# Reciprocal roots of the heads' norms: one power on GpSimd in place of a first guess and three Newton steps on VectorE

## The reference

```python
def _rms_norm(t):
    ms = jnp.mean(t * t, axis=-1, keepdims=True)
    return t * jax.lax.rsqrt(ms + RMS_EPS)
...
h = _layernorm(x, axis=-1) * (1 + ca) + sa
q, k, v = ...        # 16, 4 and 4 heads of 16 channels
q = _rms_norm(q)
k = _rms_norm(k)
attn = softmax(q k^T * scale)
y = attn v
vn = v / jnp.maximum(jnp.linalg.norm(v, axis=-1, keepdims=True), L2_EPS)
y = y - jnp.sum(y * vn, axis=-1, keepdims=True) * vn
x = x + ga * (y Wo)
h = _layernorm(x, axis=-1) * (1 + cb) + sb
x = x + gb * ffn(h)  # 8 experts, those with the top 0.9 of the probability
```

## Time and profile before

| | |
|---|---|
| median of 3 runs | 515.72 us (515.63 to 517.07) |
| profiled execution | 515.67 us, span 513.9 us |
| PE busy | 459.1 us, 89% of the span |
| DVE busy | 340.0 us, 66% |
| ACT busy | 257.9 us, 50% |
| POOL busy | 196.4 us, 38% |

### The profile page before, as it was taken

The page is one execution under the profiler, slowest core; times in us unless marked ns, Lnnn a source line. Parts: engine busy times, 40 slices in busy tenths (PEclk is TensorE's granted clock), DMA queues, the critical chain, the costliest instruction groups (busy, mean ns, idle before and its releaser), DMA issues. The chain is left out here.

```text
span 513.9 us, 9827 instructions
## 1 busy us (share of the span) xinstructions
PE 459.1 (89%) x3390; PEld 346.9 (67%) x3390; DVE 340.0 (66%) x789; ACT 257.9 (50%) x355; POOL 196.4 (38%) x233
## 2 busy tenths in 40 slices
PE   3855998999999999999998999989998999999982
PEld 3433334344444444443898999989997999999982
DVE  3388577469857986768899857764743847555451
ACT  2313677975787588777543243444422525333330
POOL 1036204002100210002243575655754665676644
PEclk9966799999999999999999898999999999999997
DMA  8500231921001100213346347774653674454443
GB/s 267 193 1 0 51 76 17 111 39 41 2 1 42 43 1 1 84 37 99 115 119 192 64 106 187 189 202 96 176 104 63 133 169 74 106 83 107 75 73 41
DMA packets 30784, 46.00 MB, mean 89 GB/s; under 512 B 3588, under 2 KB 22276, under 8 KB 30728
## 3 DMA queue, kind: packets, MB, share of 16 engines
q0 software_dynamic: 11936, 22.50, 24.1%
q1 hardware_dynamic: 18792, 22.77, 13.8%
HBM read 34.44 MB, written 12.93 MB: 92 GB/s over the span
## 5 line engine op out<-in xcount | busy, mean ns | idle before, releaser
L609 ACT ACTIVATE probs<-psS 128x1024 f32<-128x1024 f32 x128 | 123.2, 1027 | 23.9 <-PE psS L1403 23.4
L1636 PE MATMUL psS<-hs_hi,w_hi 128*128 128x256 f32 x400 | 115.4, 288 | 5.7 <-DVE hs_lo L1194 3.2
L1636 PE MATMUL psS<-hs_hi,w_lo 128*128 128x256 f32 x400 | 113.9, 285 | 0.0
L1636 PE MATMUL psS<-hs_lo,w_hi 128*128 128x256 f32 x400 | 113.8, 285 | 0.0
L474 POOL DMA_INDIRECT out<-y_sel,idx_out x44 | 77.4, 1759 | 36.2 <-DVE y_sel L1231 24.7
L1636 PEld LDWEIGHTS psS<-hs_hi,w_hi 128*128 128x128 f32 x400 | 77.0, 193 | 7.6 <-issue 7.6
L1636 PEld LDWEIGHTS psS<-hs_lo,w_hi 128*128 128x128 f32 x400 | 76.9, 192 | 0.0
L1636 PEld LDWEIGHTS psS<-hs_hi,w_lo 128*128 128x128 f32 x400 | 76.7, 192 | 0.0
L460 POOL DMA_INDIRECT h_sel<-h_rows,idx_in x50 | 54.0, 1080 | 53.1 <-DVE sel L1200 21.7
L1502 PE MATMUL psY<-probs,v_aug 128*32 128x512 f32 x512 | 69.3, 613 | 0.0
L395 POOL COPY parted<-parted 128x512 f32<-128x512 f32 x16 | 10.0, 627 | 135.8 <-DVE parted L848 135.8
(11 more groups left out here) (200 smaller groups left out, 725.8 us busy)
## 6 DMA issues: line engine op xcount, KB each, us to landing
w_in<-gateT SPq DMA_DIRECT2D x8, 512.0 KB, 4.8
w_in<-upT SPq DMA_DIRECT2D x8, 512.0 KB, 3.5
w_in<-downT SPq DMA_DIRECT2D x8, 512.0 KB, 4.4
h_rows<-h_nat SPq DMA_DIRECT2D x4, 528.0 KB, 3.5
x_all<-x SPq DMA_DIRECT2D x4, 512.0 KB, 5.4
h_rows<-mod_table POOLq DMA_DIRECT2D x4, 512.0 KB, 14.7
out<-x_all SPq DMA_DIRECT2D x4, 512.0 KB, 3.0
mod_rows<-mod_table SPq DMA_DIRECT2D x3, 512.0 KB, 5.0
```

The costliest lines, as they stand in the source:

```text
L609: act.activation(probs[:, gk % 4, 2 * pair:2 * pair + 2, :], psS[:, pair, :, :], ACT.Exp, scale=ATT_SCALE).then_inc(probs_done, 1)
L1636: mm = pe.matmul(ps[:, i * SW:(i + 1) * SW], w, v[:, k, :], start=at == 0, stop=at == 3 * KC - 1)
```

## The change

`reciprocal_roots` becomes `floor_norms`: DVE makes only the two small operations that scale the mean and set the floors. Then GpSimd raises all 96 columns to the power -0.5 in one instruction, with a tile `minus_halves` of as many exponents, and DVE's `split_heads` waits for it. GpSimd has the power ahead of the doubling of the same batch's parts.

```diff
-            def reciprocal_roots(b):
-
+            def floor_norms(b):
 
                 dve.tensor_scalar(norms[:, :, 0:HG], norms[:, :, 0:HG], 1.0 / D, RMS_EPS,
-                                  ALU.mult, ALU.add).then_inc(newton_step, 1)
+                                  ALU.mult, ALU.add).then_inc(floored, 1)
                 dve.tensor_scalar(norms[:, :, HG:ALLH], norms[:, :, HG:ALLH], L2_EPS_SQUARED, None,
-                                  ALU.max).then_inc(newton_step, 1)
-                z, y, t = (norms[:, :, :].rearrange("p t h -> p (t h)"), rnorm[:, :, :].rearrange("p t h -> p (t h)"),
-                           newton[:, :])
-                at = b * 13 + 2
-                dve.wait_ge(newton_step, at)
-                dve.tensor_scalar(t.bitcast(I32), z.bitcast(I32), 1, None, ALU.logical_shift_right).then_inc(newton_step, 1)
-                dve.wait_ge(newton_step, at + 1)
-                dve.tensor_scalar(y.bitcast(I32), t.bitcast(I32), -1.0, float(0x5f3759df), ALU.mult,
-                                  ALU.add).then_inc(newton_step, 1)
-                for step in range(3):
-                    dve.wait_ge(newton_step, at + 3 * step + 2)
-                    dve.tensor_tensor(t, y, y, ALU.mult).then_inc(newton_step, 1)
-                    dve.wait_ge(newton_step, at + 3 * step + 3)
-                    dve.scalar_tensor_tensor(out=t, in0=t, scalar=-0.5, in1=z, op0=ALU.mult, op1=ALU.mult).then_inc(newton_step, 1)
-                    dve.wait_ge(newton_step, at + 3 * step + 4)
-                    dve.scalar_tensor_tensor(out=y, in0=t, scalar=1.5, in1=y, op0=ALU.add, op1=ALU.mult).then_inc(newton_step, 1)
-                dve.wait_ge(newton_step, at + 11)
-
+                                  ALU.max).then_inc(floored, 1)
...
         def _(pool):
             pool.sem_inc(out_listed, 1)
+            pool.memset(minus_halves[:, :], -0.5).then_inc(halves, 1)
...
+            def roots(n):
+                pool.wait_ge(halves, 1)
+                pool.wait_ge(floored, 2 * n + 2)
+                pool.tensor_tensor(rnorm[:, :, :].rearrange("p t h -> p (t h)"), norms[:, :, :].rearrange("p t h -> p (t h)"),
+                                   minus_halves[:, :], ALU.pow).then_inc(rooted, 1)
+
+            roots(0)
             for tt in range(TT):
                 double_parts(0, tt)
...
             for b in range(LAST):
+                roots(b + 1)
                 double_parts(b + 1, 0)
                 double_parts(b + 1, 1)
...
                 hi, lo = parted[:, tt, :, 0, :], parted[:, tt, :, 3, :]
+                dve.wait_ge(rooted, n + 1)
                 dve.wait_ge(q_turned, 2 * m + 2)
```

More of the change, by code:

```diff
@@ L164, in adaln_block @@
         rnorm = sb("rnorm", [P, TT, ALLH])
-        newton = sb("newton", [P, TT * ALLH])
+        minus_halves = sb("minus_halves", [P, TT * ALLH])
         vn = sb("vn", [P, 2, TT, G, D])
@@ L219, in adaln_block @@
         w_loaded = [sem(f"w_loaded{n}") for n in range(3)]
-        (zeroed, ident_done, v_ones, consts, silu_step, modc_ps, modc_done, modr_ps, row_copied, mod_out, gates_in, mod_in, gate_step,
+        (zeroed, halves, ident_done, v_ones, consts, silu_step, modc_ps, modc_done, modr_ps, row_copied, mod_out, gates_in, mod_in, gate_step,
          modr_done) = sems(
-            "zeroed ident_done v_ones consts silu_step modc_ps modc_done modr_ps row_copied mod_out gates_in mod_in gate_step "
+            "zeroed halves ident_done v_ones consts silu_step modc_ps modc_done modr_ps row_copied mod_out gates_in mod_in gate_step "
             "modr_done")
         (bn1_done, ln1_stats, ln1_eps, ln1_rstd, mods_done, xhat_done, xT_ps, hT_done, qkv_ps, qkv_sb, squared, sq_sum,
-         newton_step, v_done, w_ordered, normed, hi_done, lo_done, parts_done, q_turned, k_turned, trq_done, tr_done,
+         floored, rooted, v_done, w_ordered, normed, hi_done, lo_done, parts_done, q_turned, k_turned, trq_done, tr_done,
          trk_done) = sems(
             "bn1_done ln1_stats ln1_eps ln1_rstd mods_done xhat_done xT_ps hT_done qkv_ps qkv_sb squared sq_sum "
-            "newton_step v_done w_ordered normed hi_done lo_done parts_done q_turned k_turned trq_done tr_done trk_done")
+            "floored rooted v_done w_ordered normed hi_done lo_done parts_done q_turned k_turned trq_done tr_done trk_done")
         (scores, probs_done, pv_done, y_sb, yback_ps, rden_done, yn_done, prod_done, dots_done, along_done, y_done) = sems(
@@ L949, in _ @@
             square_sums(0)
-            reciprocal_roots(0)
+            floor_norms(0)
             dve.wait_ge(modr_ps, 2)
@@ L983, in body @@
                 take_sums(b, 0)
-                reciprocal_roots(b + 1)
+                floor_norms(b + 1)
                 split_heads(b + 1, 1 - parity, 0)
```

## The result

The changed kernel takes 572.48 us (median of 4 runs, 570.70 to 575.46) against 515.67 us of the kernel before: 1.1113 times as long, with a 95% interval of 1.1069 to 1.1157 (the ratios here are as recorded for each comparison; the quotient of the two medians can differ from them by up to 0.002, here it is 1.1102). The forecast was 568.7 with a range of 550 to 584.

The account below looks back on a forecast made before the run. The four places were held to be bound by DVE's uncovered stretch from floors to first product; 47.0 us of added stretches plus 6.0 us of PE's low clock made 53 us on 515.67, 568.7 us, range 550 to 584.

Parts of the forecast that it names:

- What bounds the four places: Opening and batches 0 to 2: DVE's stretch from floors to first product, about 3.15 us each, has no cover to speak of.
- The handoff: DVE's floor to GpSimd's start, and GpSimd back to DVE, at each of four calls: about 0.1 us each way.
- The length of the power: GpSimd's power of 128x96 at each of four calls: 14.7 us, a straight line at 0.148 us per column.
- Nothing covers it: At all four calls none of the 11.75 us added per call is covered by other work: 47.0 us.
- PE's clock: Behind the new idle stretches of batches 0, 1 and 2 PE runs at half clock: 2.0 us each, 6 us, bounds 0 and 10.2.
- The sum: Whole kernel: 47.0 us of added stretches plus 6.0 us of clock, 53 us on 515.67, 568.7 us; chance 0.74.
- Flat power: GpSimd's wide power costs hardly more than a narrow one: 2.38 us, 2.3 us gained in all, 513.4 us; chance 0.05.
- Half the slope: GpSimd's power costs 0.074 us per column behind the twelfth: 8.5 us per power, 544 us in all; chance 0.08.
- Part given back: PE or ACT works ahead during the stall and 4 us of each call return: 553 us; chance 0.04.
- The dear power: GpSimd's power costs up to 26.5 us at each of four calls: 616 us in all; chance 0.04.
- The clock low through a batch: PE's clock stays low through one batch, whose 20 us of work behind the wait takes twice as long: 589 us; chance 0.05.
- The Trainium skill's figure: About 0.2 us of streaming for a 96-column GpSimd operation, estimated from an add; the swap would win some 11 us.

Follow-up runs that it names:

- the filling: Changed kernel with PE running extra matmuls into an idle bank during the waits of batches 0 to 2: 592.86 us with 34, 570.25 with 18, 567.10 with 21.
- the product: Changed kernel with GpSimd's power replaced by a product of two constant tiles over 96 columns, so every root is 0.3: 509.94 us.
- The run in tiles: Changed kernel with the power cut into four of 24 columns, each started once its tile's sums and floors are there: 516.76 us.
- The run with 18 matmuls: Changed kernel with PE running 18 extra matmuls into an idle bank during the waits of batches 0, 1 and 2: 570.25 us.
- the run with 21: Changed kernel with PE running extra matmuls into an idle bank during its waits, 18 in batch 0 and 21 in batches 1 and 2: 567.10 us.

## Why the prediction was right, and where it was off

*What bounds the four places: right.* The stretch from the floors to the first product was on the chain in all of them. PE's added waits, 12.8, 13.1 and 12.9 us, answer to 12.7, 13.1 and 12.7 us of added stretch.

*The handoff: right in size.* Forecast 0.1 + 0.1, measured 0.15 + 0.08 in the opening and 0.15 + 0.03 in batch 0; in batch 1 the start came 0.53 us behind the floor, which I can't explain; the stretch of batch 1 was longer than the others by 0.4 us in the runs with the filling and with the product too.

*The length of the power: the term that was off.* Forecast 14.7 (the profile was to show 14 to 15.5), measured 15.67. The straight line was right, its slope wasn't: two widths near to each other, the narrow one with a spread of 1.01 to 1.21, gave 0.148 us per column, and over 84 more columns the missing 0.011 makes 1 us. All seven widths that the runs had (4, 12, 16, 20, 24, 48 and 96 columns: 1.10, 2.28, 2.90, 3.58, 4.28, 8.03 and 15.67 us) lie on 0.40 + 0.159 per column to within 0.1 us; nothing bends. Four calls: 51.2 us in place of 47.0.

*Nothing covers it: right.* Up to the landmark no step of the ledger gives anything back but 0.19 us. The run in tiles shows that cover was to be had, by another order.

*PE's clock: right in kind and, by luck, in size.* Forecast 6 us (bounds 0 and 10.2), measured 5.4 by filling and 5.6 by the ledger, but spread as 0.5, 3.1 and 2.0 over batches 0, 1 and 2, not 2.0 in each. In batch 0 the kernel before waits 1.29 us for GpSimd ahead of the next turn, and in the changed kernel that turn, at 105.54, has no wait: the low clock hides in that, and only 0.5 us are left of it. Behind batch 1's stall the projection is dense, and the clock fell once more, to 0.74 on average from 189 to 192 us and 0.69 from 192 to 195, with no wait of PE ahead of it: what PE ran there last, from 188.41 to 190.36, were the router's 16 narrow matmuls of eight columns, which in the kernel before brought no fall. Of batch 1's 3.05 us 1.64 are in the projection, and the rest, 1.4 us, answers to this second fall, so it isn't surely the stall's own. The run with 18 matmuls has such a fall too, a batch later, behind the router's 16 matmuls there (252.24 to 254.19 us), and the run with 21 has none; why it comes in some runs alone stays open. What I had not seen is that far shorter waits do the same (five Newton steps).

*The sum.* 47 + 6 = 53 against 56.8 in the medians: +4.2 from the power's slope, -0.4 from the clock. The profiled spans differ by 56.0 us only; the other steps of the ledger, the start, the opening's rest and the expert part, make -0.8.

*The rivals.* Flat power: excluded by 15.67 us. Half the slope: excluded by 0.159 in place of 0.074. Part given back: half the columns returned 28.6 of 30.6. The dear power: no. The clock low through a batch: no, it was back within about 5 us of PE's return. The Trainium skill's figure (GPSIMD Engine Reference, Elementwise — side-by-side cycle accounting; an estimate of 0.2 us for 96 columns, without the fixed part) is below the 0.346 us that the product of 96 columns took in these runs, and of its order; the power, at 15.67 us, isn't such an operation.

## What to carry to other kernels

An operation on GpSimd is priced by its own rows at two widths, as far apart as there are, and not by another operation of the same shape: the product took 0.35 us, the power 15.7. A slow operation that must stay is cut so that its pieces start as soon as their inputs are there; here that took away the whole loss to within the noise (1.0009 times the kernel before, 0.9986 to 1.0032) with no less work on the engine. And a wait that is added to PE is priced with what the clock takes behind it: two more Newton steps cost 10 us where their own durations made 7.

## What the runs showed of the hardware that I had not expected

GpSimd's power costs 0.159 us per column of 128 partitions plus about 0.4 us, from 4 to 96 columns. PE's granted clock fell from its upper to its lower level over waits of 2.95 us twice and of 2.50 us once, and held over waits of 2.32 us (the 18 matmuls' run, batch 2) and 1.2 us, so that I can't give a length that parts them; the projection behind such a fall took 1.4 to 3.0 us longer, whether the wait had been 3 or 14 us long. It also fell with no wait ahead, once in the changed kernel and once in the 18 matmuls' run, right behind the router's 16 matmuls of eight columns, which in the kernel before and in the 21 matmuls' run brought no fall.
